# Feed-forward weights quantised in pairs on VectorE alone, and a block order of its own for each engine

## What is computed

```
def _w8a8_linear(x, w, b):            # rows of x and of w each have a scale max|.|/127
    return einsum(qx, qw) * (sx * sw) + b
def _xattn(x, cond, mask):            # 16 heads of 32
    q = w8a8(x, wq, bq); k = cond @ wk.T + bk; v = cond @ wv.T + bv
    o = softmax(q k^T / sqrt(32) + mask) v
    return w8a8(o, wo, bo)
def _ffn(x):                          # w_gate, w_up: 1408 x 512, w_down: 512 x 1408
    each row of x and of every weight is scaled by max|.|/448 and rounded to fp8 e4m3
    t = silu(x w_gate^T) * (x w_up^T)
    return t w_down^T                 # t quantised in the same way
x = x + tanh(g_xattn) * _xattn(layernorm(x), ctx, mask)
x = x + tanh(g_ffn)   * _ffn(layernorm(x))
```

## Time and profile before

| | us |
|---|---|
| median of 3 runs | 719.29 |
| lowest and highest | 715.14 to 721.9 |
| the profiled execution | 715.44 |
| its span, first to last instruction | 713.7 |
| prologue, to the first instruction of step 0 on DVE | 24.5 |
| step 0, step 1 | 74.8, 84.1 |
| steps 2 to 7, each | about 67.6 |
| steps 8 and 9 together | 125 |

### The profile page before, as it was taken

The page is one execution under the profiler, slowest core; times in us unless marked ns, Lnnn a source line. Parts: engine busy times, 40 slices in busy tenths (PEclk is TensorE's granted clock), DMA queues, the critical chain, the costliest instruction groups (busy, mean ns, idle before and its releaser), DMA issues.

```text
span 713.7 us, 10918 instructions
## 1 busy us (share of the span) xinstructions
PE 522.9 (73%) x3200; PEld 327.8 (46%) x3200; DVE 590.2 (83%) x1478; ACT 468.1 (66%) x1163; POOL 269.4 (38%) x243
## 2 busy tenths in 40 slices
PE   2664778448799788788968896899789875855644
PEld 2553446335564465346635653565456343422211
DVE  2777698976889998999898889889897997687692
ACT  2354487757778688678876886778677867771240
POOL 2347775400235154413623261336143513532220
PEclk9985758758999999989989998999899988978755
DMA  9313622433023102400230122022202200000000
GB/s 296 116 49 100 189 62 89 111 97 104 1 59 90 45 31 60 133 16 27 72 111 31 34 71 89 31 50 70 74 31 60 59 1 30 1 1 30 1 0 29
DMA packets 52107, 45.55 MB, mean 64 GB/s; under 512 B 7888, under 2 KB 42704, under 8 KB 52048
## 3 DMA queue, kind: packets, MB, share of 16 engines
q1 hardware_dynamic: 45504, 31.48, 16.0%
q0 software_dynamic: 3488, 12.85, 5.7%
q10 hardware_dynamic: 3056, 0.54, 0.5%
HBM read 23.87 MB, written 4.19 MB: 39 GB/s over the span
## 4 chain that ended last, share of the span: by engine, by line
DVE 42%; PE 23%; issue 14%; ACT 11%; DMA 4%; SPq 3%; POOL 1%; ACTq 1%; DVEq 0%; POOLq 0%
PE bank_g L869 6%; DVE prob L1048 5%; DVE t_sb L934 4%; DVE ts L1220 4%; DVE lo L971 3%; DVE t_sb L989 3%; SPq L294 3%; PE bank_t L698 2%; DMA bv_row<-in_L_xattn_bv_dram 2%; ACT prob L525 2%; PE bank_g L847 2%; DVE gate L1100 2%; PE bank_u L847 2%; DVE wf_max L1113 2%; DMA t_sb<-in_L_ffn_w_down_dram 1%
## 5 line engine op out<-in xcount | busy, mean ns | idle before, releaser
L525 ACT ACTIVATE prob<-prob,neg_max 128x256 f32<-128x256 f32 x256 | 127.3, 500 | 40.7 <-DVE neg_max L1048 40.7
L1048 DVE CUSTOM_DVE_ANT_0 prob<-bank_s,mask_sb 128x256 f32<-128x256 f32 x256 | 97.2, 419 | 14.5 <-PE bank_t L698 8.2
L698 PE MATMUL bank_t<-ident,prob 128*128 128x128 f32 x512 | 83.4, 288 | 29.4 <-ACT prob L525 29.3
L385 POOL TENSOR_TENSOR up<-up,wu_scale 128x512 f32<-128x512 f32 (+1 forms) x42 | 53.0, 1262 | 107.4 <-ACT up L510 106.4
L535 ACT ACTIVATE probT<-bank_t 128x512 f32<-128x512 f32 x128 | 74.7, 583 | 16.3 <-PE bank_o L736 10.9
L388 POOL TENSOR_TENSOR up<-gate,up 128x512 f32<-128x512 f32 (+1 forms) x48 | 66.1, 1377 | 45.5 <-DVE gate L1100 24.0
L698 PEld LDWEIGHTS bank_t<-ident,prob 128*128 128x128 f32 x512 | 62.2, 148 | 41.9 <-ACT prob L525 40.3
L869 PE MATMUL bank_g<-wdT,turned 128*128 128x512 bf16 x176 | 60.0, 510 | 19.0 <-DVE turned L1073 19.0
L392 POOL TENSOR_TENSOR x<-x,qf 128x512 f32<-128x512 f32 x14 | 17.9, 1277 | 116.3 <-DVE qf L1233 116.3
L847 PE MATMUL bank_g<-wgT,x2T 128*128 128x512 bf16 (+1 forms) x192 | 47.5, 371 | 13.7 <-DVE gate L1100 12.2
L934 DVE SCALAR_TENSOR_TENSOR t_sb<-mag,t_sb 128x512 f32<-128x512 f32 (+1 forms) x60 | 52.8, 891 | 4.7 <-ACT t_sb L452 3.6
(11 more groups left out here) (200 smaller groups left out, 1294.8 us busy)
## 6 DMA issues: line engine op xcount, KB each, us to landing
x_in<-in_x_dram SPq DMA_DIRECT2D x8, 512.0 KB, 3.6
c_in<-in_ctx_dram SPq DMA_DIRECT2D x8, 512.0 KB, 3.4
kk<-hi SPq DMA_DIRECT2D x64, 64.0 KB, 2.0
kk<-lo SPq DMA_DIRECT2D x64, 64.0 KB, 2.0
qq<-hi SPq DMA_DIRECT2D x64, 64.0 KB
...
```

Of the source, the lines that this page charges most:

```text
L385: pool.tensor_tensor(up[:, c % 2, 0:w], up[:, c % 2, 0:w], wu_scale[:, off:off + w], ALU.mult).then_inc(s["u_scaled"], 1)
L525: ins = act.activation(prob[:, head_par, t, :], prob[:, head_par, t, :], ACT.Exp, bias=neg_max[:, head_par, t:t + 1], scale=-1.0, accum_ou ...
L698: ins = pe.transpose(T_BANK[1 - hp][:, lc * N + t * P:lc * N + (t + 1) * P], prob[:, 1 - hp, t, lc * P:(lc + 1) * P], ident[:, :])
L1048: ins = dve.tensor_tensor_reduce(prob[:, hp, t, :], S_BANK[hp][:, t * L:(t + 1) * L], mask_sb[:, hb, t, :], -1.0, 3.4e38, ALU.add, ALU.min ...
```

## The change

It has four parts.

1. **Units in pairs.** The 26 units become 15: chunk `c` of `w_gate` and of `w_up` form one unit of 128x1024 (`pair`), and `w_down` keeps its four. Two `w_down` units come first: unit 0 in the prologue, unit 1 in slot 0. From then on a unit starts every second slot. The stages ("hops") of unit `k` lie at slots 2k-2 (scale, DVE), then at the same slot on ACT, one slot later rounding (DVE), two later turning (PE), three later copying out (ACT).
2. **Who does what.** POOL no longer rounds; DVE rounds all units. DVE no longer copies units out of PSUM; ACT does (`copy_unit`). The multiplications with the identity are gone (`diag_w`, `diag`, and those of `wo`): PE takes the scale, broadcast, as its stationary operand. One reciprocal gives both inverses. The raw pairs take turns in three buffers (`gate`, `x2`, the first row of `t_sb`); `mag` holds one whole unit.
3. **Loads.** POOL loads `w_down` unit 0 first, unit 1 after `x_in` has landed, then pairs, two to three units ahead. ACT's queue issues gates and bias rows first. The waits for the small loads move out of the prologue on DVE (`bias_scale`, after slot 7) and on ACT (`pro_v`).
4. **Order.** The loop over slots is gone. Every block is a function, and for each kind of step (0, 1, 2 to 7, 8, 9) each engine has a written list of calls. Many lists differ from the old order by exchanges of neighbours, some by moves over several blocks. In step 1 the second half of the turned o goes to `O_BANK`, not `U_BANK`.

```diff
+        UNITS = [("down", 0), ("down", 1)] + [("pair", c) for c in range(IC)] + [("down", r) for r in range(2, CC)]
+        def unit_at(u, first):
+            k = (u - first) // 2 + 1
+            return [k] if (u - first) % 2 == 0 and 0 <= k < W_UNITS and u >= 0 else []
...
+            def load_unit(k):
+                kind, n = UNITS[k]
+                if kind == "down":
+                    pool.dma_start(unit_raw(k), w_down[n * P:(n + 1) * P, :]).then_inc(unit_loaded(k)[0], 16)
+                else:
+                    for m, src in enumerate((w_gate, w_up)):
+                        pool.indirect_dma_start(pair_raw[n % 3][:, m * C:(m + 1) * C], None, src,
+                                                bass.IndirectOffsetOnAxis(ap=index[:, n:n + 1], axis=0)).then_inc(unit_loaded(k)[0], 16)
+            load_unit(0)
+            pool.wait_ge(s["x_loaded"], 16)
+            load_unit(1)
             pool.wait_ge(s["index_loaded"], 16)
+            load_unit(2)
+            load_unit(3)
...
-                            pool.tensor_scalar(m, m, M_LEAST, None, ALU.max).then_inc(s["mag_floored"], 1)
-                            pool.wait_ge(s["mag_floored"], v // 2 + 1)
-                            pool.tensor_tensor(raw, m, raw, ALU.add).then_inc(s["pool_sum_ready"], 1)
-                            pool.wait_ge(s["pool_sum_ready"], v // 2 + 1)
-                            pool.wait_ge(s["q8_ready"], v)
-                            pool.tensor_tensor(unit_q(v), m, raw, ALU.subtract).then_inc(s["q8_ready"], 1)
...
+            def mag_unit(k):
+                act.wait_ge(s["wf_scaled"], 4 * k + 4)
+                need(act, s["wf_ready"], k)
+                raw = unit_raw(k)
+                if UNITS[k][0] == "pair":
+                    for n in range(2):
+                        act.activation(mag[:, n, :], raw[:, n * C:(n + 1) * C], ACT.Abs, scale=wf_r[:, k % 3, 1, n:n + 1])
+                    for n in range(2):
+                        ins = act.activation(raw[:, n * C:(n + 1) * C], raw[:, n * C:(n + 1) * C], ACT.Copy, scale=wf_r[:, k % 3, 0, n:n + 1])
...
+            def copy_unit(k):
+                kind, n = UNITS[k]
+                act.wait_ge(s["wf_turned"], k + 1)
+                if kind == "pair":
+                    act.activation(wguT[:, :, :, n * P:(n + 1) * P], half(G_BANK).rearrange("p (m c o) -> p m c o", m=2, c=CC), ACT.Copy)
+                    ins = act.activation(wgu_scale[:, :, n * P:(n + 1) * P], U_BANK[:, 2 * P:4 * P].rearrange("p (m o) -> p m o", m=2), ACT.Copy)
...
+            def turn_unit(k):
+                need(pe, s["wf_out"], k)
+                pe.wait_ge(s["wf_scaled"], 4 * k + 2)
+                for n in range(unit_cols(k)):
+                    pe.matmul(U_BANK[:, (2 + n) * P:(3 + n) * P], wf_s[:, k % 3, 0, n:n + 1].to_broadcast([P, P]), ident[:, :],
+                              start=True, stop=True, skip_group_check=True)
+                pe.wait_ge(s["wf_ready"], k + 1)
...
+            def scale_unit(k):
+                n, b2, k0 = unit_cols(k), k % 3, 4 * k
+                dve.wait_ge(*unit_loaded(k))
+                need(dve, s["wf_turned"], k - 2)
+                raw = unit_raw(k) if n == 1 else unit_raw(k).rearrange("p (m c) -> p m c", m=2)
+                dve.tensor_reduce(wf_max[:, b2, 0:n], raw, AX.X, ALU.max, apply_absolute_value=True).then_inc(s["wf_scaled"], 1)
+                dve.wait_ge(s["wf_scaled"], k0 + 1)
+                dve.tensor_scalar(wf_s[:, b2, 0, 0:n], wf_max[:, b2, 0:n], 1.0 / 448.0, None, ALU.mult).then_inc(s["wf_scaled"], 1)
+                dve.tensor_scalar(wf_s[:, b2, 1, 0:n], wf_max[:, b2, 0:n], 1.0 / 448.0 / TWO20, None, ALU.mult).then_inc(s["wf_scaled"], 1)
+                dve.wait_ge(s["wf_scaled"], k0 + 3)
+                dve.reciprocal(wf_r[:, b2, :, 0:n], wf_s[:, b2, :, 0:n]).then_inc(s["wf_scaled"], 1)
+            def round_unit(k):
+                raw, dst, parts = unit_raw(k), unit_q(k), unit_parts(k)
+                dve.wait_ge(s["wf_mag"], k + 1)
+                for lo_, hi_, m in parts:
+                    dve.scalar_tensor_tensor(raw[:, lo_:hi_], m[:, 0:hi_ - lo_], M_LEAST, raw[:, lo_:hi_], ALU.max, ALU.add).then_inc(s["wf_sum"], 1)
...
+                    ins = dve.scalar_tensor_tensor(dst[:, lo_:hi_], m[:, 0:hi_ - lo_], M_LEAST, raw[:, lo_:hi_], ALU.max, ALU.subtract)
...
             scale8("q", 0)
+            scale_unit(0)
             pro_evac("k")
             int8("q", 0)
-            dve.wait_ge(s["small_loaded"], 64)
...
-            dve.wait_ge(s["row_loaded"], 32)
-            dve.wait_ge(s["tanh_ready"], 1)
...
+            round_unit(0)
             pro_evac("q")
```

The lists of calls, here those of DVE in step 0 and of PE and DVE in steps 2 to 7 (the number is the slot that the block had):

```diff
+                if b == 0:
+                    x_stats(0); unit_scale(0); pro_v(2); x_scales(2); unit_scale(2); unit_round(3); pro_int_o(4)
+                    k_low_0(3); unit_scale(4); k_low_1(4); xT_low(5); unit_round(5); pro_o(5); unit_scale(6)
+                    sx_copy(7); bias_scale(3); q_scale_0(7); unit_round(7); q_low_0(8); q_low_1(9); unit_round(9)
+                    unit_scale(8); unit_scale(10); unit_round(11); v_evac(11); head_mask(12); head_mask(13)
+                    unit_scale(12); unit_round(13); head_mask(14); head_mask(15); v_evac(12); unit_scale(14)
+                    unit_round(15)
...
+                elif b < NB:
+                    head_score(0); oqT_turn(0); head_score(1); ctxT_turn(0); head_turn(0); y_project(0); head_turn(1)
+                    ctxT_turn(1); group_pv(1); head_score(2); head_turn(2); k_project(2); head_score(3); head_turn(3)
+                    k_project(3); head_turn(4); head_score(4); xT_turn(4); head_score(5); head_turn(5); group_pv(5)
+                    x2T_turn(5); head_score(6); xT_turn(5); gate_up_project(5); head_turn(6); gate_up_project(6)
+                    sx_turn(6); q_project_0(6); head_score(7); head_turn(7); gate_up_project(7); q_project_1(7)
+                    head_score(9); head_score(8); head_turn(8); gate_up_project(8); head_turn(9); group_pv(9)
+                    gate_up_project(9); head_turn(10); v_project(10); head_score(10); gate_up_project(10)
+                    v_project(11); head_turn(11); first_score(11); tT_turn(11); head_score(12); head_turn(12)
+                    down_project(12); head_score(13); head_turn(13); head_score(14); group_pv(13); tT_turn(13)
+                    head_turn(14); o_turn(14); head_turn(15); down_project(14); head_score(15)
...
+                elif b < NB:
+                    x_stats(0); head_mask(0); oqT_low(0); head_mask(1); y_scale(1); head_mask(2); x_scales(2)
+                    x2_stats(2); head_mask(3); x2_scales(3); head_mask(4); k_low_0(3); x2_fp8_0(4); x2_fp8_1(4)
+                    k_low_1(4); head_mask(5); xT_low(5); x2T_copy(5); head_mask(6); gate_scale(6); head_mask(7)
+                    gate_scale(7); sx_copy(7); t_mul(7); q_scale_0(7); head_mask(8); gate_scale(8); q_low_0(8)
+                    t_mul(8); head_mask(9); gate_scale(9); t_mul(9); q_low_1(9); t_scales(9); head_mask(10)
+                    gate_scale(10); t_mul(10); t_fp8_0(10); head_mask(11); v_evac(11); gate_scale(11); t_mul(11)
+                    t_fp8_0(11); t_mul_last(11); t_scales(11); head_mask(12); tT_low(12); v_evac(12); t_fp8_1(12)
+                    head_mask(13); t_fp8_1(13); y2_scale(13); head_mask(14); tT_low(14); o_norm(14); head_mask(15)
+                    o_norm(15); o_scales(15); y2_scale(15)
```

1300 lines of the change are left out of this document (681 added, 619 removed).

## The result

The changed kernel takes 692.15 us in the median (689.79 to 695.15), the kernel before 717.34 on the same chip (715.14 to 721.9). The ratio is 0.964, with a 95% interval of 0.958 to 0.971. Timed again later, beside some of the experiments, it took 691.42 against 721.12, a ratio of 0.961 (0.956 to 0.966). The forecast was 681 in a range of 664 to 702. The time lies in the range, 11 us above the forecast, and on the 692 of rival A.

The account below looks back on a forecast made before the run. DVE's work bounds steps 2 to 7 (91% busy); weight work makes step 1 longest. Step 0 -10, step 1 -14.5, prologue 0, steps 2 to 7 -12, drain -2: 719.3 - 38.5 = 681 us, range 664 to 702.

Parts of the forecast that it names:

- rival A: Whole kernel: the weights gain, the order does not; steps 2 to 7 give 2.4, drain nothing; 692 us, chance 0.23.
- Pairs and division of work in steps 0 and 1: Steps 0 and 1: less DVE weight work; step 0 -10 to 65 us, step 1 -14.5 to 69.5 us.
- Rival C: Step 1: ACT or the single `mag` takes the gain back, step stays at 88 us; 695 us, chance 0.12.
- ACT as the fullest engine of step 1: Step 1: ACT busy 62 us, ahead of DVE; at 91% the step takes 68, taken as 69.5.
- DVE's durations: Steps 0 and 1: rounding 1024 columns 1.23 us; DVE busy about 52 and 54 us; stretched small instructions gone.
- Waits for `w_down`: Step 1: DVE's 4.6 us of waits for the last two loads go, each load issued at least two units ahead.
- Prologue: Before step 0: zero change, between -2 and +2 us; unit 0's load and DVE work against waits removed.
- Steps 2 to 7: Six steps: new order saves a quarter of DVE's idle time, 1.6 a step, 2 with `diag`: -12 us.
- Drain: Steps 8 and 9: an ACT multiplication and one gate scaling come earlier, -2 us.
- B: Steps 2 to 7: the order gains more, idle falls to 2 us a step; 666 us, chance 0.15.
- D: Steps 2 to 7: slower, the order fits badly; at 6 us lost a step 731 us, chance 0.04.
- E: Steps 0 and 1: the change in the weights does nothing, they are chains and not work; 719 us, chance 0.04.

Follow-up runs that it names:

- unit0_after_x: Changed kernel with POOL issuing the load of `w_down` unit 0 only when x has landed; 694.04 us, a single time.
- the five kernels with the same lists: Changed kernel (twice), and it with steps 0-1 in slot order, bias loads on SP, or unit 0 loaded after x; steps 2 to 6: 67.5 to 68.6 us.
- steady_slot_order: Changed kernel with the lists of steps 2 to 9 put back into slot order on every engine; 695.34 us.

## Why the prediction was right and wrong

- **Pairs and division of work in steps 0 and 1: total right, split wrong.** Forecast -24.5, found -29.2 and -25.6 in two profiles. But the working derived it from busy times, ACT's in step 1 and DVE's in step 0, and gave the order nothing there. In slot order the same work gives -15.8; that the order brought the missing 10 to 13 was luck. The step that failed is the one from busy time to length: "At the 91% that DVE reaches in steps 2 to 7". In slot order step 1 takes 74.5 with ACT busy 60.1 (81%) and DVE 56.1 (75%), because each waits for the other; with the written lists it takes 65.6 with ACT at 87%. Rival C, given 0.12, had the two engines holding each other up, though by the single `mag`, which costs 2.7 us. The lists call some of ACT's multiplications a block or more earlier (that of slot 0 of step 1, and those of slot 8) and some of DVE's roundings a block or two later (in step 1 those of slots 5 and 7). The distance of the two matters: in the code ACT multiplies unit k at slot 2k, two slots after its scale and not in the same slot as "The change" says, and DVE rounds it at 2k+1, PE turns it at 2k+2, ACT copies it out at 2k+3.
- **ACT as the fullest engine of step 1: place right, size wrong.** Forecast 62 us, measured 57.3, less than the 58.9 before. The prices held (2.9, 1.01, 0.38). The count did not: the multiplications took 18.3 us in this window, that is two whole `w_down` units at 3.5 and about four pairs, where five were counted, and one `w_down` unit less was copied out. The lists had moved these blocks over the window's edge.
- **DVE's durations: right.** 1.23 forecast for a rounding of 1024 columns, 1.22 measured; busy 54 forecast in step 1, 51.7 measured, since three pairs and not four were scaled in it; 52 in step 0, 55.2 measured, where one small instruction took 1.89 us and one rounding 2.04. So stretched instructions are gone from step 1, where the earlier trace rows had one of 1225 ns (the longest on two columns is now 0.17), but not from step 0, in which POOL has 20.5 us of work left. POOL's 74 us of the two steps went to 26.8, and did not "nearly vanish".
- **Waits for `w_down`: right.** Those of the earlier trace rows are gone; one of 2.5 us for a pair's load is new.
- **Prologue: wrong by 2.5 us.** The range of -2 to +2 was derived from the 16 DMA engines' rate, and `wq` landed 1.2 us later (7.74 against 6.54). But the path goes over ACT's queue: an issue that waits there keeps ACT from its first instruction. The working looked at DVE's list (its wait of the earlier trace rows did go) and at bandwidth, not at ACT's queue, although the change reorders it. The rule of the Trainium skill ("DMA: Bandwidth & Descriptors", "Issuing engines are not separate DMA queues") on DMAs that interleave, cited in the prediction, would have given 2 us for the load in front; for `wq` it was 0.2 (`unit0_after_x`).
- **Steps 2 to 7: wrong, +0.6 a step instead of -2.** The 0.6 is within the spread of the five kernels with the same lists; the missing 2 are not. Six steps of it are 16 us, more than the 11 between forecast and result; that the better steps 0 and 1 paid for the rest, so that the time lies in the range, was luck. The failed step is "I take a quarter of the idle time". Of the two named waits one fell (6.9 to 2.2 us over five steps, for the gate) and the other rose (5.3 to 10.9, for the turns of heads), and DVE's idle time rose from 6.2 to 8.5 us a step. The working asked what each exchange releases, and not what it delays: an exponential of 1.0 us went in front of ACT's last part of k, and behind that part stands a queue that needs 10.3 us for its 16 DMAs and had no slack before. Nor is that the whole: slot order takes the exponential away again, the stack starts at 18.4 to 18.8 in steps 3 to 6, and the steps take 68.1. As rival A said, "a released wait may come back at the next block".
- **The fall of DVE's busy time there, 61.3 to 59.7, is no saving.** Of it 0.4 is `diag`. Most of the rest is one operation, `lo` of q, four times a step; its groups over steps 3 to 6, before and then after:

```profile
L971 DVE SCALAR_TENSOR_TENSOR lo<-qf,bq_col,hi 128x256 f16<-128x256 f32 x16 | 15.8, 1027 | 2.2 <-ACT hi L574 2.2
```

```profile
L1112 DVE SCALAR_TENSOR_TENSOR lo<-qf,bq_col,hi 128x256 f16<-128x256 f32 x16 | 11.1, 732 | 7.1 <-ACT hi L616 7.1
```

  The same instruction is 295 ns shorter, 1.2 us a step, and DVE idles 1.2 us a step more in front of it. Busy time was waiting in disguise, and 1.2 of the 2.3 us by which DVE's idle time rose are no new loss. In `steady_slot_order` it is 1013 ns again. The trace shows where the stretch comes from. DVE and POOL in order of time, step 4 of the kernel before:

```profile
352.87 1.27 POOL L385 TENSOR_TENSOR up<-up,wu_scale 128x512 f32<-128x512 f32 x1 [0.83 <-ACT up L510]
352.91 2.92 DVE L971 SCALAR_TENSOR_TENSOR lo<-qf,bq_col,hi 128x256 f16<-128x256 f32 x2
354.21 1.33 POOL L388 TENSOR_TENSOR up<-gate,up 128x512 f32<-128x512 f32 x1
```

  and of the changed kernel:

```profile
324.98 0.88 DVE L1112 SCALAR_TENSOR_TENSOR lo<-qf,bq_col,hi 128x256 f16<-128x256 f32 x2 [1.77 <-ACT hi L616]
...
329.30 1.89 DVE L1112 SCALAR_TENSOR_TENSOR lo<-qf,bq_col,hi 128x256 f16<-128x256 f32 x2
329.63 1.28 POOL L367 TENSOR_TENSOR up<-up,wgu_scale 128x512 f32<-128x512 f32 x1 [1.19 <-ACT up L542]
```

  An instruction that DVE starts while one of POOL's products runs ends 0.28 us after that product, here after 1.49 us; one that starts before POOL's or beside none takes 0.47 to 0.49. In steps 3 to 6 eight of the sixteen were stretched to 1.49 or more before and four to 0.6, and four to 1.49 after. The Trainium skill ("SBUF — State Buffer", "SBUF: two separate sides") describes a port pair that goes to whichever of GpSimd and VectorE starts first, for its whole instruction, when VectorE's has two inputs from SBUF and GpSimd's reads SBUF. The rows agree with that.
- **Drain: -2 forecast, -1.5 found** (124.5 to 123.0 from the end of step 7), and the kernel with its drain in slot order, 7.9 us longer from step 7 on, ran at a lower clock there too.
- **Rivals.** A was the nearest: steps 2 to 7 gave nothing, and the time is its 692. Its premise, though, that part 1 alone gives the 24.5, is not what the runs show. B did not occur either, since DVE's idle time rose. D did not: no order tried cost a step more than 1.4 us. E did not: steps 0 and 1 gave 25.6 us or more.
